# Sums over the channels in four 32-column tiles of TensorE, and one more matmul to add them

## What is computed

```python
h = tok(x)
h = h + attn(_layernorm(h))        # norm 0
h = h + ffn_nf4(_layernorm(h))     # norm 1
h = h + ssm(_layernorm(h))         # norm 2
h = h + lora_moe(_layernorm(h))    # norm 3

def _layernorm(x, axis=-1, eps=1e-05):
    m = jnp.mean(x, axis=axis, keepdims=True)
    v = jnp.var(x, axis=axis, keepdims=True)
    return (x - m) / jnp.sqrt(v + eps)

# in lora_moe
base = xf @ W_base.T + b_base
logits = xf @ W_router.T
rw, sel = jax.lax.top_k(logits, 2)
rw = softmax(rw)
```

## Time and profile before

| | us |
|---|---|
| median of 3 runs | 4660.4 |
| lowest, highest | 4654.24, 4661.36 |
| the profiled execution | 4655.0 |
| its span, first to last instruction | 4653.2 |
| PE busy | 4288.1 (92%) |
| DVE busy | 2944.0 (63%) |
| ACT busy | 1925.1 (41%) |
| POOL busy | 2374.1 (51%) |

### The profile page before, as it was taken

The page is one execution under the profiler, slowest core; times in us unless marked ns, Lnnn a source line. Parts: engine busy times, 40 slices in busy tenths (PEclk is TensorE's granted clock), DMA queues, the critical chain, the costliest instruction groups (busy, mean ns, idle before and its releaser), DMA issues.

```text
span 4653.2 us, 61881 instructions
## 1 busy us (share of the span) xinstructions
PE 4288.1 (92%) x23384; PEld 2834.9 (61%) x23408; DVE 2944.0 (63%) x3095; ACT 1925.1 (41%) x2873; POOL 2374.1 (51%) x1017
## 2 busy tenths in 40 slices
PE   0886999999999999999999999999999999999999
PEld 0654777754457777754357777754457777754457
DVE  7896546459953446459953446459953536469953
ACT  1111223467732223467732223367732223367731
POOL 3443333358863333358863333358863333368862
PEclk9898999999998999999998999999998999999998
DMA  1113222310022222320022222310022222310021
GB/s 41 37 37 124 71 72 71 121 65 16 14 73 85 86 69 68 121 65 16 14 73 86 84 71 68 121 65 16 14 76 83 86 69 72 121 63 14 16 75 64
DMA packets 95229, 302.70 MB, mean 65 GB/s; under 512 B 11408, under 2 KB 15632, under 8 KB 92688
## 3 DMA queue, kind: packets, MB, share of 16 engines
q1 hardware_dynamic: 85776, 282.62, 18.6%
q10 hardware_dynamic: 9216, 16.78, 1.0%
HBM read 253.22 MB, written 46.14 MB: 64 GB/s over the span
## 4 chain that ended last, share of the span: by engine, by line
PE 81%; DVE 13%; issue 2%; ACT 1%; POOL 1%; DMA 1%; SPq 0%; DVEq 0%; ACTq 0%; POOLq 0%
PE psg L823 38%; PE psx L998 9%; PE psg L1013 7%; DVE sb_wst L1492 6%; PE psg L850 5%; PE psx L838 3%; PE psg L859 2%; PE psx L805 2%; PE psx L929 1%; PE psg L1027 1%; PE psg L812 1%; PE psx L942 1%; PE psg L975 1%; PE psx L1040 1%; PE psg L1024 1%
## 5 line engine op out<-in xcount | busy, mean ns | idle before, releaser
L505 POOL TENSOR_TENSOR sb_wl<-sb_raw,sb_wh 128x1024 fp32r<-128x1024 f32 x388 | 973.0, 2511 | 1841.1 <-ACT sb_wh L572 1841.0
L1492 DVE TENSOR_TENSOR_SCAN sb_wst<-sb_dA,psx 128x1024 f32<-128x1024 f32 x512 | 1140.2, 2271 | 37.7 <-ACT sb_dA L695 23.7
L998 PEld LDWEIGHTS psx<-sb_dgB,sb_duT 64*128 64x128 f32 x4096 | 359.2, 189 | 526.2 <-DVE sb_wst L1492 263.6
L695 ACT ACTIVATE sb_dA<-sb_dlt,sb_a_sb 128x504 f32<-128x504 f32 x1024 | 646.4, 704 | 60.6 <-DVE sb_wst L1492 54.8
L998 PE MATMUL psx<-sb_dgB,sb_duT 64*128 64x256 f32 x4096 | 591.9, 409 | 85.7 <-DVE sb_wst L1492 83.9
L572 ACT ACTIVATE sb_wh<-sb_raw 128x1024 fp32r<-128x1024 f32 x388 | 408.2, 1053 | 616.5 <-PE psg L823 330.8
L539 POOL TENSOR_TENSOR sb_wst<-sb_wst,sb_cb_lo 128x1024 f32<-128x1024 f32 x256 | 599.4, 2364 | 90.2 <-DVE sb_wst L1492 90.1
L539 POOL TENSOR_TENSOR sb_wst<-sb_wst,sb_cb_hi 128x1024 f32<-128x1024 f32 x256 | 598.2, 2357 | 76.2 <-DVE sb_wst L1492 76.2
L1013 PE MATMUL psg<-sb_wst,sb_cst 64*64 64x512 f32 x4096 | 564.3, 624 | 10.3 <-POOL sb_wst L539 9.6
L823 PE MATMUL psg<-sb_xh,sb_wh 128*128 128x512 f32 x2112 | 557.9, 407 | 0.0
L823 PE MATMUL psg<-sb_xh,sb_wl 128*128 128x512 f32 x2112 | 522.2, 389 | 0.0
(11 more groups left out here) (250 smaller groups left out, 5823.1 us busy)
## 6 DMA issues: line engine op xcount, KB each, us to landing
sb_raw<-in_w SPq DMA_DIRECT2D x360, 512.0 KB, 3.3
sb_raw<-w_ffn_dequantized SPq DMA_DIRECT2D x32, 512.0 KB, 3.3
gates<-sb_gt ACTq DMA_DIRECT2D x64, 256.0 KB, 2.5
sb_gin<-gates SPq DMA_DIRECT2D x64, 256.0 KB, 2.7
h_after_tok<-sb_hT SPq DMA_DIRECT2D x4, 2048.0 KB, 14.6
sb_u<-h_after_tok SPq DMA_DIRECT2D x4, 2048.0 KB, 8.1
h_after_tok<-sb_h SPq DMA_DIRECT2D x4, 2048.0 KB, 8.4
sb_h<-h_after_tok SPq DMA_DIRECT2D x4, 2048.0 KB, 7.9
```

The lines of the kernel that those rows point to most:

```text
L505: pool.tensor_tensor(rest(b, i0), raw[:, i0 % RAW, :, :], high(b, i0).bitcast(F32), ALU.subtract).then_inc(s_wl, 1)
L695: ins_ = A(dA[:, (m * NQ + k) % RING, :, n, 1:S], dlt[:, m % 2, :].rearrange("p (b s) -> p b s", b=NB)[:, :, 1:S], ACT.Exp, scale=a_sb[:, ...
L998: ins_ = mm(psx[:, 2 * j + r, :].rearrange("p (a t e) -> p a t e", a=8, e=2)[:, :, :, e], duT[r0:r0 + 64, m % 2, i * P:(i + 1) * P], dgB[r ...
L1492: v.tensor_tensor_scan(wst[:, x, 4 * j:4 * j + 4, :, :].rearrange("p b n s -> p (b n s)"), dA[:, x, 4 * j:4 * j + 4, :, :].rearrange("p b ...
```

## The change

Three sums over the channels are made in another way. Where a 128x128 f32 matrix took one slice after the other, a helper `over_tiles` now issues four matmuls of 32 output columns each, for four slices, whose results stand in partitions 0 to 31, 32 to 63, 64 to 95 and 96 to 127 of one bank; then four more for the other four slices, into the same places. So a bank holds four partial sums. They are added by one more step: ACT copies the bank to `tA` (`s_sqc`, `s_fmc`), and one f32 matmul with the old 1/1024 matrix adds all 128 rows (`variance`, `mean_fold`). The weights of 1/32 make the factor right. `sq` gets four buffers, and `stat` acts at every fourth slice only.

The router's sums go the same way with `wr` padded to 32 columns: experts by tokens, in four parts. DVE multiplies them by `rstd` into `tB`, and four matmuls with `tB` as weights and an 8-column matrix `pick8` add the parts and turn them to tokens by experts in `psx` bank 3. They stand behind base strip 0; the routing's transposes now stand behind base strip 1, and the next block's mean between them and base strip 2. The three LoRA products come after base strip 2, and `mean_fold` after them.

```diff
-                    if k >= 2:
-                        act.wait_ge(s_squ, b * LNU + L * KC + k - 1)
-                    A(sq[:, k % 2, :], xc[:, k, :], ACT.Square).then_inc(s_sq, 1)
-                act.wait_ge(s_squ, b * LNU + L * KC + KC)
+                    if k == 4:
+                        act.wait_ge(s_squ, 8 * b + 2 * L + 1)
+                    A(sq[:, k % 4, :], xc[:, k, :], ACT.Square).then_inc(s_sq, 1)
+                act.wait_ge(s_squ, 8 * b + 2 * L + 2)
+                A(tA[:, :], psx[:, 1, :], ACT.Copy).then_inc(s_sqc, 1)
+                act.wait_ge(s_var, 4 * b + L + 1)
...
+            def mean_copy(b):
+
+                act.wait_ge(s_fm, b + 1)
+                A(tA[:, :], psx[:, 0, :], ACT.Copy).then_inc(s_fmc, 1)
...
+                    if b == 0:
+                        mean_copy(0)
                     for i in range(AHEAD):
                         split(b, i)
                     norm(b, 0)
...
                     norm(b, 3)
                     split(b, BASE0 + 1)
+                    split(b, BASE0 + 2)
...
-                    for i in range(BASE0 + 2, NSTRIP):
+                    if b + 1 < nblk:
+                        mean_copy(b + 1)
+                    for i in range(BASE0 + 3, NSTRIP):
                         split(b, i)
...
+            def over_tiles(bank, weights, x, k):
+
+                for c in range(4):
+                    ins_ = mm(psx[32 * c:32 * c + 32, bank, :], weights(k + c), x(k + c), start=(k == 0), stop=(k == 4))
+                return ins_
+
             def stat(b, L, k):
 
-                pe.wait_ge(s_sq, b * LNU + L * KC + k + 1)
-                mm(psx[:, 1, :], C("mean"), sq[:, k % 2, :], start=(k == 0), stop=(k == KC - 1)).then_inc(s_squ, 1)
+                if k % 4 == 3:
+                    pe.wait_ge(s_sq, b * LNU + L * KC + k + 1)
+                    over_tiles(1, lambda n: C("over32"), lambda n: sq[:, n % 4, :], k - 3).then_inc(s_squ, 1)
+
+            def variance(b, L):
+
+                pe.wait_ge(s_sqc, 4 * b + L + 1)
+                mm(psx[:, 1, :], C("mean"), tA[:, :], start=True, stop=True).then_inc(s_var, 1)
...
+                        if s == 1 and L is not None and k == 4:
+                            variance(b, L)
...
-                for k in range(KC):
-                    ins_ = mm(psx[:, 0, :], C("mean"), u[:, k, :], start=(k == 0), stop=(k == KC - 1))
-                ins_.then_inc(s_mean, 1)
+                for k in (0, 4):
+                    ins_ = over_tiles(0, lambda n: C("over32"), lambda n: u[:, n, :], k)
+                ins_.then_inc(s_fm, 1)
...
-                    for t in range(T // P):
-                        for k in range(KC):
-                            ins_ = mm(psx[:, 2, t * NEXP:(t + 1) * NEXP], xc[:, k, t * P:(t + 1) * P], wr[:, k, :],
-                                      start=(k == 0), stop=(k == KC - 1))
+                    for k in (0, 4):
+                        ins_ = over_tiles(2, lambda n: wr[:, n, :], lambda n: xc[:, n, :], k)
...
-                    pe.wait_ge(s_rstd, b + 1)
+                    base(0)
+                    pe.wait_ge(s_lg, b + 1)
                     for t in range(T // P):
-                        ins_ = mm(psx[:, 3, t:t + 1], rstd[:, t * P:(t + 1) * P], C("ident", 0, 1), start=True, stop=True)
+                        ins_ = mm(psx[:, 3, t * NEXP:(t + 1) * NEXP], tB[:, t * P:(t + 1) * P], C("pick8"), start=True, stop=True)
...
                     v.wait_ge(s_rout, b + 1)
+                    tt(tB[:, :], psx[:, 2, :], rstd[:, :], ALU.mult).then_inc(s_lg, 1)
                     v.wait_ge(s_rT, b + 1)
-                    rT = rt[:, 7, 0:T // P]
-                    own.link(v.tensor_copy(rT, psx[:, 3, 0:T // P]))
-                    own.link(tt(by_e(lg), by_e(psx[:, 2, 0:T // P * NEXP]), spread(rT), ALU.mult))
+                    own.link(v.tensor_copy(lg, psx[:, 3, 0:T // P * NEXP]))
```

More of the change, by code:

```diff
@@ L82, in constants @@
     put("rms", rms)
+    put("over32", np.full((P, 32), 1.0 / 32))
+    put("pick8", np.arange(P)[:, None] % 32 == np.arange(NEXP)[None, :])
     put("eps_ln", np.full((P, 1), 1e-5))
@@ L165, in tower @@
         a_sb = sb("a_sb", [P, DC * NST])
-        wr = sb("wr", [P, KC, NEXP])
+        wr = sb("wr", [P, KC, 32])
         conv = sb("conv", [P, DC, TAPS + 3])
@@ L226, in tower @@
             with ExitStack() as c2:
-                sq = sb("sq", [P, 2, T], F32, c2)
+                sq = sb("sq", [P, 4, T], F32, c2)
                 tA = sb("tA", [P, T], F32, c2)
@@ L318, in tower @@
         s_xfree = sem("s_xfree")
+        s_sqc, s_var, s_fm, s_fmc, s_lg = sem("s_sqc"), sem("s_var"), sem("s_fm"), sem("s_fmc"), sem("s_lg")
         CR_STRIP, CR_WL, CR_UPD, CR_CONV, CR_U, CR_GT = 1, 2, 4, 4, 2, 4
@@ L865, in first_mean, with mean_fold @@
                 pe.wait_ge(s_h, 16 * b + 16)
-                for k in range(KC):
-                    ins_ = mm(psx[:, 0, :], C("mean"), u[:, k, :], start=(k == 0), stop=(k == KC - 1))
-                ins_.then_inc(s_mean, 1)
+                for k in (0, 4):
+                    ins_ = over_tiles(0, lambda n: C("over32"), lambda n: u[:, n, :], k)
+                ins_.then_inc(s_fm, 1)
+            def mean_fold(b):
+                pe.wait_ge(s_fmc, b + 1)
+                mm(psx[:, 0, :], C("mean"), tA[:, :], start=True, stop=True).then_inc(s_mean, 1)
             def norm(b, L):
@@ L892, in _ @@
                         first_mean(0)
+                        mean_fold(0)
                     for j in range(KC + 1):
@@ L1132, in _ @@
                         pe.wait_ge(s_xl, b * LNU + 3 * KC + k + 1)
+                        if k == 4:
+                            variance(b, 3)
                         ins_ = mm(psg[:, 3, :], wh[:, slot(b, LA0), k, :], xl[:, k, :], start=False, stop=(k == KC - 1))
                     ins_.then_inc(s_strip, 1)
-                    pe.wait_ge(s_rstd, b + 1)
-                    for t in range(T // P):
-                        ins_ = mm(psx[:, 3, t:t + 1], rstd[:, t * P:(t + 1) * P], C("ident", 0, 1), start=True, stop=True)
-                        if t == 0:
-                            ins_.then_inc(s_strip, 1)
-                    ins_.then_inc(s_rT, 1)
                     def base(m):
@@ L1153, in _ @@
                     base(0)
+                    pe.wait_ge(s_lg, b + 1)
+                    for t in range(T // P):
+                        ins_ = mm(psx[:, 3, t * NEXP:(t + 1) * NEXP], tB[:, t * P:(t + 1) * P], C("pick8"), start=True, stop=True)
+                        if t == 0:
+                            ins_.then_inc(s_strip, 1)
+                    ins_.then_inc(s_rT, 1)
+                    base(1)
                     pe.wait_ge(s_w16, b + 1)
@@ L1157, in _ @@
                     ins_.then_inc(s_wTm, 1)
-                    base(1)
                     if b + 1 < nblk:
                         first_mean(b + 1)
+                    base(2)
                     pe.wait_ge(s_hwl, b + 1)
                     pe.wait_ge(s_wl, b * NSTRIP + LB0 + 1 + CR_WL)
-                    lora(0)
-                    lora(1)
-                    for m in range(2, KC):
+                    for m in range(3):
+                        lora(m)
+                    if b + 1 < nblk:
+                        mean_fold(b + 1)
+                    for m in range(3, KC):
                         base(m)
@@ L1325, in norm @@
                     own.link(tt(rsin[:, :, :], over_b("sin"), r, ALU.mult))
-                if L == 3:
-                    v.sem_inc(s_rstd, 1)
             def scaled(b, at, x):
@@ L1350, in add_loop @@
                     start_sum(b, L)
-                if which == 1 and b + 1 < nblk:
-                    v.wait_ge(s_mean, 4 * b + 5)
                 for m in range(KC):
@@ L1370, in add_loop @@
                         if which == 1 and b + 1 < nblk:
+                            if m == 0:
+                                v.wait_ge(s_mean, 4 * b + 5)
                             centre(b + 1, 0, m)
@@ L1566, in _ @@
                     norm(b, 3)
-                    own = Own(v, s_own["route"], b * 20)
+                    own = Own(v, s_own["route"], b * 19)
                     def by_e(a):
@@ L1601, in _ @@
                     own.link(tt(o1, o1, o2, ALU.add))
-                    assert own.n == 20, own.n
+                    assert own.n == 19, own.n
                     v.tensor_copy(w16[:, :, :].rearrange("p t (e r) -> p t e r", r=RANK),
@@ L1642, in laid_out @@
         "a": n["L1_attn_A"].reshape(DC, P, NST).transpose(1, 0, 2).reshape(P, DC * NST),
-        "wr": n["L1_ffn_W_router"].T.reshape(KC, P, NEXP).transpose(1, 0, 2),
+        "wr": np.pad(n["L1_ffn_W_router"].T.reshape(KC, P, NEXP).transpose(1, 0, 2), ((0, 0), (0, 0), (0, 32 - NEXP))),
         "conv": conv.reshape(DC, P, TAPS + 3).transpose(1, 0, 2),
```

## The result

The changed kernel takes 4600.7 us (median of 4 runs, 4596.8 to 4602.7) against 4658.6 for the kernel before (4 runs). The ratio is 0.9875, with a 95% interval of 0.9858 to 0.9893: 58 us less. The direction was forecast and the time lies in the range, but the forecast was 4582 and the sum behind it 75.5 us. So the question of this part is where 18 to 23 us of gain stayed: 18 in the medians, 23 in the two profiled executions, whose spans went from 4653.2 to 4600.9.

What follows compares the result with a forecast made beforehand. PE was taken as the bound, busy 4288.1 of 4653.2 us. Gains 17.2 - 3 - 5 + 4 x 13.8 + 3 x 3.7 = 75.5 off 4655.0 gave 4579.5; forecast 4582, range 4562 to 4630.

Steps and rivals of the forecast that it cites:

- The price of a group: Four f32 matmuls side by side on PE: 1.05 us taken, bounds 0.86 and 3.44.
- Rival B: Four tiles of 128 rows don't run side by side: 4660 to 4700, chance 0.06; milder form 4606 to 4625, 0.07.
- (a): Norms 1 and 2, eight of them: first phase gains 3.1, summing matmul takes 0.95 back; 2.15 each, 17.2 us.
- (b): Norm 0 of blocks 1 to 3: Ln, on the path, comes 1.0 us later; cost 3 us in all.
- (c): Norm 0 of block 0: ACT's copy of the mean sums stands ahead of weight splits; cost about 5 us, once.
- (d): Router and what follows, four blocks: gain 13.8 us each, with a new wait of 0.9 before the transposing matmuls.
- rival D: Transposing wait long because a split holds up VectorE twice, 2 to 3 us a block: 4590; within the forecast's 0.55.
- (e): Next block's mean, three times: 6.87 us becomes 2.1 + 0.95; gain 3.7 each.
- Rival A: TensorE's clock falls in the norms' thinned slices, about 2.8 us a norm, nearer 3.7 in norm 0: 4597 to 4632, chance 0.24.
- C: More gain than forecast: VectorE no longer meets POOL in norm 0, first phases gain more: 4555 to 4567, chance 0.08.

Runs made afterwards that it cites:

- e9: The change with six buffers for the squares instead of four, the two new ones taken from the convolution: 4573.2 us, ratio 0.9828.
- e7: The change with the summing matmul of norms 0 to 2 behind six matmuls of strip 1 instead of ten: 4597.8 us, ratio 0.9871.
- e0: The same changed kernel run once more, nothing edited: 4598.9 us, ratio 0.989.
- e4: The change with its norms' part taken out (old squares and two buffers), router and means as changed: 4591.9 us, ratio 0.9866.
- e2: The kernel before with the router's part alone, including the earlier split of base strip 2: 4592.5 us, ratio 0.9874.
- e3: The kernel before with the next block's mean alone in groups (first mean too): 4648.3 us, ratio 0.9986.
- e6: The change with ACT's split of base strip 2 waiting for the product of logits and rstd: 4596.1 us, ratio 0.9876.
- e10: The kernel before with one line: in norm 0 ACT splits strip 3 only when rcos and rsin are written: 4627.5 us, ratio 0.9938.
- e8: e4 with one more ACT wait: in norm 0 strip 3 is split only after rcos and rsin are made: 4575.6 us, ratio 0.9827.

## Why the prediction was right, and where it failed

**The price of a group was right**, 0.90 to 1.04 at full clock against 1.05 taken, and 1.6 to 1.9 at half. Rival B fell with it: four tiles of 128 rows do run side by side. The Trainium skill ("TensorE: Matmul & The Clock Gate", "Part 3: Packing small matmuls — row/col tiling") ties the overlap of a weight load with running matmuls to another row group. The trace disagrees: a group takes 0.90, nearly the 0.86 of a single f32 matmul, and not four times that.

**(a) is the step that failed.** 17.2 was forecast for norms 1 and 2, and about 1 came. Two inputs of its sum were wrong. The first is the baseline. "Norms 1, 2 and 3 start with the half clock and look like rows 2" was read from one block; the window above has norm 1 of block 0 at 1.00 throughout, and so it was in three of four blocks. At full clock the old first phase is eight slices of 1.32 and ends 11.6 us behind the first xh, not 14.5, so in norm 1 there was little to take. In norm 2 of three blocks it ended at 13.2. The second is the wait at the fifth square, sized at 1.4 and measured at 2.17 in norms at the half clock. With it group 2 ends 11.7 to 12.0 us behind the first xh, where my sum had 11.3, and the summing matmul's 0.87 comes on top. e9 shows the size of this: without the wait norms 1 and 2 give another 14. That this with what was there is nearly the forecast is chance, since the baseline was still wrong. (By its own rows the sum should have had 3.3 for the first phase where it says 3.1, and 3.8 for each mean where it says 3.7; nothing hangs on it.)

**(b) was right in its rows and the cost did not show.** Ln 1.0 later: 14.0 us behind the first xh instead of 13.0. PE's wait for qs: 6.0 instead of 3.73, "about 6" in the text. The three segments are -0.5 together, not +3. In block 1 qs is indeed 1.0 late, and PE is 1.6 quicker from there to norm 1; the windows of that stretch show that the clock fell for less long at a later wait (0.83 instead of 0.75 over 20 us). Whether this is more than chance was not shown; in e7, which ran the same stretch 0.9 sooner, it was at 0.74.

**(c)** was 5, of which 2.2 lay ahead of the first xh. Norm 0 of block 0 alone is 5.3 longer, and 6.3 in e0. The start is +3.2 and -3.1 in these two executions of the same kernel, so its 2.2 can't be told from chance, and (c) was sized somewhat too low.

**(d)** Router 9.1 instead of 8.8, first phase 2.8 instead of 3.1, and in block 0 the clock stayed at 1.00 behind it as forecast:

```profile
1448.20:1460.10 11.90, 9.34 (x46) 6.36 (x38) 7.37 (x5) 3.22 (x4) 5.24 (x2) 1.00 0.16 49
```

The term that was mis-sized is the wait, 0.9 a block: it is 2.6, since both of VectorE's last steps of rstd ran into POOL (2.51 and 2.75 in the chain above), where I had counted one. I named this as rival D, a split that holds up VectorE twice, priced it at 2 to 3 us a block and took 0.9 into the sum. It has a second price that I left out. In block 1 the clock fell while PE waited, in block 3 just behind the wait. Chain of block 1:

```profile
2487.05 1.88 PE psx L1185 x8
2488.92 7.70 PE psg L838 x24
```

against 1.06 and 5.59 in block 0: 2.9 us more. In block 3 the strip took 7.20, 1.6 more. Four waits of 1.7 more than planned and these two falls are 11.3, and the gap to be explained in (d) and (e) is 10.8. Block by block it fits too: blocks 0 and 2 are 1.3 and 1.7 short of the forecast, block 1 is 4.6 short and block 3 is 3.2.

**(e)** 3.7 was forecast for each mean. e4 less e2 in norm 3 gives 4.0, 2.6 and 3.8. It needs the earlier split of base strip 2, which e3 lacks.

**Rival A.** The measured 4600.7 lies in A's band (4597 to 4632, chance 0.24) and not in the forecast's own (4568 to 4596). But A is not what brought it there. The thinned slices did lose the clock, though only in norm 1 was that new, in three blocks, and not in norm 0 of blocks 1 to 3, where I feared it; by my estimate above it cost about 1 us each and not 3. The wording by which the prediction called A void does not hold here: the clock fell in slices whose longest gap was 1.60 us (below). **C** was half seen: the meeting of VectorE and POOL was put at some 2 us in each norm 0. It is 6, and one line takes it away.

## What to carry to other kernels

When PE work in a loop is thinned out, work out the other engine's pace first, with its buffers: four buffers freed together held ACT for 0.8 to 2.2 us a norm, and two more turned a rewrite that lost 7 to 9 us into one that gains 19. Read the baseline of a step in every block in which it stands, not in one. And where a chain of short VectorE steps is on the path, look at what POOL does beside it, and when you move POOL's work, at what it meets in its new place (e6).

## What the runs showed of the hardware

Two kinds of VectorE step, TENSOR_TENSOR with both inputs in SBUF and TENSOR_SCALAR from SBUF to SBUF, once they start beside a POOL subtraction, end 0.05 to 0.6 us after it, whatever their own work. In the changed kernel, norm 0 of block 1, timelines of VectorE and of POOL:

```profile
1522.80 2.51 DVE L1332 TENSOR_SCALAR sb_tA<-sb_tA 128x512 f32<-128x512 f32 x1
1525.35 2.71 DVE L1333 TENSOR_TENSOR sb_rstd<-sb_tB,sb_tA 128x512 f32<-128x512 f32 x1
...
1529.54 0.69 DVE L1440 TENSOR_TENSOR sb_qc<-psg,sb_rcos 128x512 f32<-128x512 f32 x1
1530.15 0.68 DVE L1441 TENSOR_TENSOR sb_qs<-psg,sb_rsin 128x512 f32<-128x512 f32 x1
```

```profile
1522.29 5.22 POOL L508 TENSOR_TENSOR sb_wl<-sb_raw,sb_wh 128x1024 fp32r<-128x1024 f32 x2 [17.16 <-ACT sb_wh L575]
1529.49 2.35 POOL L508 TENSOR_TENSOR sb_wl<-sb_raw,sb_wh 128x1024 fp32r<-128x1024 f32 x1 [1.98 <-ACT sb_wh L575]
```

A step that is free takes 0.43 or 0.69 (e10). The two that start inside the subtractions take 2.51 and 2.71. The products q (L1440, L1441) read one operand from a bank, and run beside the third subtraction at 0.69 and 0.68. Nor does a reduction with its one input in SBUF stall (TENSOR_REDUCE, L1621 in e6: 0.20 inside a subtraction, where L1622, a TENSOR_TENSOR of 128x32 right behind it, takes 2.02 and ends 0.05 behind the subtraction of 1452.91 to 1455.30). So it is not enough that the operands lie in SBUF, as the theory of e8 and e10 had it. That the stall goes when POOL's work moves is shown by e6, e8 and e10. The Trainium skill ("SBUF — State Buffer", "Who interferes with whom") has the reason: VectorE shares a pair of ports with POOL under an exclusive lock. An instruction with two inputs in SBUF needs it; one with at most one such input needs it only in a mode that uses both ports, which the section says `tensor_scalar` can enter and `tensor_reduce` on trn2 cannot. The rows agree, by which steps stall and by how long: not a slower step but one that waits for the whole subtraction.

The other surprise is how soon TensorE's clock falls to its lower level in short gaps. Timeline of PE in the changed kernel, norm 1 of block 0; the first record behind each gap, and one of the records behind it, which takes 0.40 at 2.4 GHz (the one at 727.01) and here, at 1.2 GHz, 0.63:

```profile
726.71 0.47 PE L877 MATMUL psg<-sb_xh,sb_wh 128*128 128x512 f32 x1 [1.60 <-ACT sb_xh L583]
...
727.65 0.50 PE L877 MATMUL psg<-sb_xh,sb_wh 128*128 128x512 f32 x1 [0.25 <-ACT sb_xh L583]
...
728.70 0.80 PE L877 MATMUL psg<-sb_xh,sb_wh 128*128 128x512 f32 x1 [0.31 <-ACT sb_xh L583]
729.29 0.63 PE L877 MATMUL psg<-sb_xh,sb_wl 128*128 128x512 f32 x1
```

It fell behind one gap of 1.60 us and two of 0.25 to 0.31. It also fell in two of the four waits of 2.6 us in the changed kernel, and in all four of e9. The price was 1.6 to 2.9 us where PE led, and by the estimate above about 1 us in norm 1.
